# GpSimd rotates q and k of the first layer from two biased copies made by ScalarE

## What is computed

```python
def rotate_half(x):                       # pairs (even, odd) -> (-odd, even)
    return stack((-x[..., 1::2], x[..., ::2]), -1).reshape(x.shape)

xn = layernorm(x)
# layer 1: causal attention, 16 heads of 16, rotary position embedding
Q, K, V = (heads(xn @ W.T + b) for W, b in ((Wq, bq), (Wk, bk), (Wv, bv)))
Q = Q * cos + rotate_half(Q) * sin
K = K * cos + rotate_half(K) * sin
attn = softmax(where(causal, Q @ K.T / 4, -inf)) @ V
# and a gated low-rank mixture: router top 2 of 32, rank 16 each
x = x + attn @ Wo.T + bo + moe(xn)
xn = layernorm(x)
# layer 2: no bias, no rotation; scores times a 0/1 mask (masked keys keep weight exp(0)); a linear
# branch on a second normalisation with the signs of the weights
x = x + attn2(xn) + (layernorm(xn) @ sign(W).T) * scale * gamma + beta
```

## Time and profile before

| | before |
|---|---|
| median of 3 runs | 1581.62 us (1579.21 to 1581.71) |
| the profiled execution | 1581.71 us, its span 1580.0 us |
| instructions | 26931 |
| TensorE matmul busy | 1498.6 us (95%) |
| TensorE weight load busy | 794.9 us (50%) |
| VectorE busy | 1138.0 us (72%) |
| ScalarE busy | 853.8 us (54%) |
| GpSimd busy | 239.0 us (15%) |
| granted TensorE clock, mean | 0.977 of 2.4 GHz |

### The profile page before, as it was taken

One profiled execution on the slowest core, in us unless ns is written; L12 is line 12 of the kernel. 1 busy time (PEld: TensorE's weight loads), 2 busy tenths in 40 slices (PEclk: granted clock), 3 DMA queues, 4 the chain that ended last, 5 costly groups with the idle time before them and its releaser, 6 DMA issues.

```text
span 1580.0 us, 26931 instructions
## 1 busy us (share of the span) xinstructions
PE 1498.6 (95%) x10398; PEld 794.9 (50%) x10398; DVE 1138.0 (72%) x2546; ACT 853.8 (54%) x1661; POOL 239.0 (15%) x196
## 2 busy tenths in 40 slices
PE   4599999999999999999999999999999999999998
PEld 3345445564546544554445644556444554446444
DVE  7788887777675677567887768877776677785851
ACT  1115545556665755666355445454756576664674
POOL 6211202002011302013020021110302131201000
PEclk9779999999999999999999989999999999999999
DMA  5114030030304022230400502004021300304000
GB/s 181 40 41 82 2 81 2 2 81 2 81 2 81 2 43 41 50 85 1 81 2 2 134 1 64 19 1 81 2 48 36 77 6 2 82 2 107 3 2 27
DMA packets 44094, 66.27 MB, mean 42 GB/s; under 512 B 7328, under 2 KB 18880, under 8 KB 43968
## 3 DMA queue, kind: packets, MB, share of 16 engines
q1 hardware_dynamic: 40800, 63.77, 18.1%
q10 hardware_dynamic: 3168, 0.79, 0.2%
HBM read 9.23 MB, written 4.19 MB: 8 GB/s over the span
## 4 chain that ended last, share of the span: by engine, by line
PE 85%; DVE 7%; ACT 4%; issue 2%; POOL 1%; DMA 0%; ACTq 0%; DVEq 0%; POOLq 0%
PE WB L1033 25%; PE O L1178 18%; PE WB L1133 16%; PE ST L1158 15%; PE ST L1161 3%; PE WB L1136 3%; ACT PT L739 3%; PE WB L1186 2%; DVE mxa L971 1%; DVE rope_b L871 1%; PE WB L1194 1%; PE WB L1058 1%; PE WB L1099 1%; DVE veps L825 1%; DVE mxb L971 1%
## 5 line engine op out<-in xcount | busy, mean ns | idle before, releaser
L739 ACT ACTIVATE PT<-ST 128x512 f32<-128x512 f32 (+1 forms) x1216 | 634.5, 578 | 394.0 <-PE ST L1161 292.1
L971 DVE TENSOR_REDUCE mxa<-WB 128x1 f32<-128x512 f32 (+3 forms) x864 | 531.6, 664 | 145.7 <-PE WB L1136 97.3
L1133 PE MATMUL WB<-KS,QS 96*128 96x512 bf16 (+3 forms) x1536 | 436.2, 332 | 7.3 <-DVE attn L1005 4.3
L1158 PE MATMUL ST<-QS,KS 99*128 99x512 bf16 (+3 forms) x1536 | 429.4, 329 | 12.1 <-ACT PT L739 9.7
L1178 PE MATMUL O<-PT,Vaug 128*17 128x512 f32 (+3 forms) x3072 | 323.0, 494 | 7.2 <-ACT PT L739 4.3
L1158 PEld LDWEIGHTS ST<-QS,KS 99*128 99x128 bf16 x1536 | 144.2, 98 | 210.4 <-ACT PT L739 118.9
L971 DVE TENSOR_REDUCE mxb<-WB 128x1 f32<-128x384 f32 (+3 forms) x352 | 213.6, 635 | 36.9 <-PE WB L1136 36.1
L1133 PEld LDWEIGHTS WB<-KS,QS 96*128 96x128 bf16 x1536 | 146.0, 99 | 186.4 <-DVE mxa L971 55.3
L1136 PE MATMUL WB<-negmask,identb 128*128 128x128 bf16 x1024 | 199.8, 222 | 0.0
L1161 PE MATMUL ST<-negmaskT,identb 128*128 128x128 bf16 x1024 | 197.5, 220 | 0.0
L608 POOL TENSOR_TENSOR proj<-proj,parts 128x512 f32<-128x512 f32 x64 | 74.1, 1161 | 457.5 <-ACT parts L699 457.4
(11 more groups left out here) (139 smaller groups left out, 1351.9 us busy)
## 6 DMA issues: line engine op xcount, KB each, us to landing
QS<-parts SPq DMA_DIRECT2D x96, 256.0 KB, 5.0
KS<-parts SPq DMA_DIRECT2D x96, 256.0 KB, 5.0
x<-in_x SPq DMA_DIRECT2D x4, 1024.0 KB, 5.6
out<-x SPq DMA_DIRECT2D x8, 512.0 KB, 2.9
QS<-nmT ACTq DMA_DIRECT2D x32, 24.0 KB
w_q<-in_w_q SPq DMA_DIRECT2D x2, 256.0 KB, 6.1
w_k<-in_w_k SPq DMA_DIRECT2D x2, 256.0 KB, 6.0
cos<-in_cos SPq DMA_DIRECT2D x1, 512.0 KB, 5.5
```

Of the source, the lines that this page charges most:

```text
L739: act.activation(PT[:, q % PT_SLOTS, j:j + n, 0:wd], src, ACT.Exp, scale=float(SCALE[STAGES[k][1]])).then_inc(exp_done.sem, 1)
L971: dve.tensor_reduce(dst, bank, AX.X, ALU.max).then_inc(emptied, 1)
L1133: mm = pe.matmul(bank[:, q * wd:(q + 1) * wd], QS[0:KR, h + qb * P:h + (qb + 1) * P], KS[0:KR, h + seg * BANK:h + seg * BANK + wd], start= ...
L1158: mm = pe.matmul(ST[:, o + i * wd:o + (i + 1) * wd], KS[0:KM, h + kb * P:h + (kb + 1) * P], QS[0:KM, h + q0:h + q0 + wd], start=True, stop ...
```

## The change

28 of the 32 units of the first layer, all but the first four of k = 0 (`ROTATED`), go another way. ScalarE makes two copies of the bank, both with the bias added: one to proj, one to rope_b in two instructions of 64 partitions, crossed over; then the bank is free. GpSimd multiplies rope_b by sin and proj by cos, waits for both, and subtracts them into proj (the sine table has its sign by the half of partitions it is read from, so the addition becomes a subtraction). `first` of the unit waits for this on a new semaphore, `rotated`. As there is one rope_b, ScalarE's copies of a unit wait for the rotation of the unit before. Nothing is removed from VectorE's code: it keeps the first four units. The planner gets the new steps with costs of `ac(512) + 1200` = 1802 ns for ScalarE and 3550 ns for GpSimd.

```diff
--- before.py
+++ after.py
@@ -79,9 +79,15 @@
 W_KINDS = ("wz", "fold", "xT", "qk", "router", "v", "hU", "gT", "ffn", "later", "max", "rows", "out", "aT", "wo")
 
 
+
+ROTATED = [(k, c) for k, (_, l) in enumerate(STAGES) if l == 0 for c in range(NW) if k or c >= NW // 2]
+
+
 def emptier(step):
     if step[0] in EMPTIES_SECOND and STAGES[step[1]][1] == 1:
         return EMPTIES_SECOND[step[0]]
+    if step[0] == "qk" and step[1:] in ROTATED:
+        return "act"
     return EMPTIES.get(step[0], "dve")
 
 
@@ -148,9 +154,17 @@
             due = at(0.1 + 0.03 * c) if ot == 0 else at(0.5 + 0.05 * (c - 4))
             land = [("sp", ("stack", k, 0))] if ot else ([("sp", ("stack", k - 1, 1))] if k else [])
             job("pe", ("qk", k, c), mm(1024, 4) + 60, due, [("act", ("xT", k, 2 * hf + 1)), ("sp", ("weights", 0))], PE_LAG)
-            job(emptier(("qk", k)), ("qk", k, c), 3100 if l == 0 else ac(512), due,
-                [("pe", ("qk", k, c))] + ([("pool", ("third", k, c - 2))] if c > 1 else [("pool", ("third", k - 1, NW - 2 + c))] if k else []))
-            job("act", ("first", k, c), 640, due, [(emptier(("qk", k)), ("qk", k, c))] + land)
+            slot = [("pool", ("third", k, c - 2))] if c > 1 else [("pool", ("third", k - 1, NW - 2 + c))] if k else []
+            done = (emptier(("qk", k, c)), ("qk", k, c))
+            if (k, c) in ROTATED:
+                i = ROTATED.index((k, c))
+                used = [("pool", ("rope",) + ROTATED[i - 1])] if i else [("dve", ("qk", 0, NW // 2 - 1))]
+                job("act", ("qk", k, c), ac(512) + 1200, due, [("pe", ("qk", k, c))] + slot + used)
+                job("pool", ("rope", k, c), 3550, due, [done])
+                done = ("pool", ("rope", k, c))
+            else:
+                job(done[0], done[1], 3100 if l == 0 else ac(512), due, [("pe", ("qk", k, c))] + slot)
+            job("act", ("first", k, c), 640, due, [done] + land)
             job("pool", ("rest", k, c), 1180, due, [("act", ("first", k, c))])
             job("act", ("second", k, c), 640, due, [("pool", ("rest", k, c))])
             job("pool", ("third", k, c), 1180, due, [("act", ("second", k, c))])
@@ -459,6 +473,7 @@
         moe_logits = Signal(sem("moe_logits"))
         moe_exp = Signal(sem("moe_exp"))
         suffix_ok = Signal(sem("suffix_ok"), 6)
+        products, rotated = sem("products"), sem("rotated")
         negmax_parts = Signal(sem("negmax_parts"), NG)
         negmax_in = Signal(sem("negmax_in"), NG, step=16)
         st_full = Signal(sem("st_full"), NG * NEX)
@@ -602,6 +617,19 @@
                 row = brow[:, 1 if STAGES[k][1] == 0 else 2, :].unsqueeze(1).broadcast_to([P, NT, D])
                 pool.tensor_tensor(xs, xs, row, ALU.add).then_inc(biased.sem, 1)
 
+            def rotate(k, c):
+                kind, ot, hf = chunk(c)
+                tok = slice(hf * BANK, (hf + 1) * BANK)
+                done = ROTATED.index((k, c))
+                if done == 0:
+                    pool.wait_ge(w_in["qk"], W_IN["qk"])
+                pool.wait_ge(*empty(("qk", k, c)))
+                pool.tensor_tensor(rope_b[:, :], rope_b[:, :], sin[:, tok], ALU.mult).then_inc(products, 1)
+                pool.tensor_tensor(proj[:, c % 2, :], proj[:, c % 2, :], cos[:, tok], ALU.mult).then_inc(products, 1)
+                pool.wait_ge(products, 2 * done + 2)
+
+                pool.tensor_tensor(proj[:, c % 2, :], proj[:, c % 2, :], rope_b[:, :], ALU.subtract).then_inc(rotated, 1)
+
             def first_rest(k, c):
                 kind, ot, hf = chunk(c)
                 pool.wait_ge(*part1.upto(k, c + 1))
@@ -637,7 +665,7 @@
                 pool.tensor_tensor(ev[:, :, :], later_v[:, g * GH:(g + 1) * GH, :, :].rearrange("p h n v -> p (h n) v"),
                                    e_all[:, g, :].unsqueeze(2).broadcast_to([P, GH * NT, VA]), ALU.mult).then_inc(ev_ready.sem, 1)
 
-            run = {"wmax": largest_weight, "bias": bias, "rest": first_rest, "third": third_part,
+            run = {"wmax": largest_weight, "bias": bias, "rope": rotate, "rest": first_rest, "third": third_part,
                    "suffix": suffix_sum, "ev": later_terms}
             for s in ORDER["pool"]:
                 run[s[0]](*s[1:])
@@ -665,6 +693,21 @@
                     act.wait_ge(*part3.upto(k, c - 1))
                 else:
                     act.wait_ge(*part3.upto(k - 1, NW - 1 + c))
+                if (k, c) in ROTATED:
+                    kind, ot, _ = chunk(c)
+                    bank = bank_of(("qk", k, c))
+                    i = ROTATED.index((k, c))
+                    if i:
+                        act.wait_ge(rotated, i)
+                    else:
+                        act.wait_ge(*empty(("qk", 0, NW // 2 - 1)))
+                        act.wait_ge(w_in["first"], W_IN["first"])
+                    act.activation(proj[:, c % 2, :], bank, ACT.Identity, bias=bcol[:, kind, ot:ot + 1])
+                    for to, at in ((0, P // 2), (P // 2, 0)):
+                        half = slice(at, at + P // 2)
+                        ins = act.activation(rope_b[to:to + P // 2, :], bank[half, :], ACT.Identity, bias=bcol[half, kind, ot:ot + 1])
+                    ins.then_inc(bank_empty["act"], 1)
+                    return
                 act.activation(proj[:, c % 2, :], bank_of(("qk", k, c)), ACT.Copy).then_inc(bank_empty["act"], 1)
 
             def values(k, i):
@@ -689,7 +732,10 @@
 
             def first_part(k, c):
                 kind, ot, hf = chunk(c)
-                act.wait_ge(*empty(("qk", k, c)))
+                if (k, c) in ROTATED:
+                    act.wait_ge(rotated, ROTATED.index((k, c)) + 1)
+                else:
+                    act.wait_ge(*empty(("qk", k, c)))
                 if c == 4:
                     for turn in lane:
                         act.wait_ge(*turn.upto(k, 3))
```

## The result

The changed kernel takes 1565.82 us (median of 4 runs, 1565.65 to 1566.95), the kernel before beside it 1581.44 us (1579.21 to 1581.71): a ratio of 0.9906 [0.9889, 0.9923], 15.6 us faster. The forecast was 1577.5 us; the result lies inside the range, near its fast end and near rival (a)'s 1563. The profiled execution is one of 1565.65 us with a span of 1563.9 us.

A forecast was written before the change was run, and what follows sets the result against it. TensorE was taken as the bound, with 85% of the chain of waits; other engines count only by making it wait. The terms -6.4 - 3 + 4.8 + 0.4 = -4.2 us gave 1577.5 us, range 1563 to 1591 (8 in 10).

The forecast's parts named there:

- rival (a): VectorE was the hidden brake: start-up -6 us, whole excess -12.8 us, ScalarE's copies free; 1563 us, chance 0.18.
- ScalarE's bursts: Three extra copies in a row per unit, 24 in stages 0, 3, 4, at 0.2 us each: +4.8 us (0 to +16.8).
- Contention: GpSimd's added work holds some small VectorE instructions of the splits in stages 0, 3, 4: +0.4 us.
- VectorE's relief: Stages 0, 3, 4: VectorE loses 24 us of rotations each, TensorE's weight loads wait less: -6.4 us (0 to -12.8).
- the half: Only half the excess of weight-load waits counted as time, since loads also idle while the previous matmul streams: -6.4 us.
- 12.8 us of excess waits: Large VectorE rows of weight-load waits: 37.4 us in stages 0, 3, 4 against 24.6 us for three stages without rotations.
- equal ST rows at 51 and 64% of ScalarE: ST waits of 27.3 us (stages 1, 2) and 32.6 us (3, 4): ScalarE's busy share doesn't by itself set TensorE's waits.
- The start-up: Before the first exponential, c = 7's projection moves later and VectorE goes on with maxima: -3 us (0 to -6).
- rival (b): Slower: each of 24 copy bursts on ScalarE costs 0.7 us beyond the ST banks; +7.8 us, 1589.5 us, chance 0.20.
- The cover of GpSimd's chain: Chain to the stack some 2.3 us longer a unit, covered by 16.4 us before the k = 5 transfer: no cost.
- (c): Nothing comes of it: VectorE's time was off the path, its waits pass to ScalarE; 1581 us, chance 0.15.
- (d): GpSimd holds VectorE's two-input split instructions some 0.9 us each in stages 0, 3, 4: +11 us, 1593 us, chance 0.05.

The follow-up runs named there:

- the loads alone: Kernel before, rotation still on VectorE, plus ScalarE's three copies and GpSimd's three operations for each of 28 units on unread buffers: 1589.98 us, ratio 1.0071.
- VectorE refilled: Changed kernel plus three VectorE reductions with unread result for each of the 28 moved units: 1588.37 us, ratio 1.006.
- the kernel planned with 3400 ns: Kernel before with the planner's duration for VectorE's rotation at 3400 instead of 3100 ns, so only orders differ: 1581.14 us, ratio 1.0008.
- k = 0 alone: Kernel before with only the last four units of k = 0 rotated on GpSimd, the others on VectorE: 1576.16 us, ratio 0.9977.
- replanning with 3.95 us: Changed kernel with planned durations as measured, GpSimd's step 3950 instead of 3550 ns and ScalarE's copies 130 ns more: 1567.51 us, ratio 0.9915.
- k = 1: Kernel before with only the eight units of k = 1 rotated on GpSimd, the others on VectorE: 1583.84 us, ratio 1.0025.

## Why the prediction was right in sign and off in size

The forecast was -4.2 us and the time moved by -15.6 us. That it lies in the range is partly luck: the range's fast end was rival (a)'s 1563 us, and (a)'s terms did not come true one by one.

The runs give the terms by themselves, roughly. In the sum of the forecast ScalarE's bursts were +4.8 us; they measured +7.4 (interval 4.1 to 8.5). Contention was +0.4 us; GpSimd's presence measured some +3 to +5. VectorE's relief, start-up included, was -9.4 us; the changed kernel lies 1565.8 - 1590.0 = -24.2 us below the kernel with the loads alone and 1565.8 - 1588.4 = -22.6 us below the one with VectorE refilled. So three terms were too small, the gain by far the most.

**The mis-sized term is VectorE's relief, and the step that failed in it is the half.** I took 12.8 us of excess waits and half of them, -6.4 us, as time, because a load also waits while the matmul before it streams. The excess itself was read from the large rows only; all rows give 21.3 us before and 4.7 us after. And stages 3 and 4 together became 12.5 us shorter, net of bursts, where the forecast had -6.4 + 4.8 + 0.4 = -1.2 us for all three stages. (Stage 0's 4.4 us are hardly a gain, with 3.2 us more in the start.) Three things were outside the sum:
- *Waits in ScalarE's name were in part VectorE's.* I read equal ST rows at 51 and 64% of ScalarE as a matter between TensorE and ScalarE. With VectorE refilled the ST row rose from 30.9 to 35.5 us, of which an order alone can make 2 us. Late maxima empty a bank late, TensorE comes late to everything in its order, and has less in hand when it must wait for an exponential. This chain is my reading; the row is what was shown.
- *The clock.* In 45 runs of the unchanged kernel before, beside the experiments, those with a mean granted clock of 0.977 (six) took 1581.8 us on average, those with 0.982 (two) 1577.7 us: 0.8 us for each 0.001. The profiled before had 0.977 and the profiled after 0.982, which is some 4 of their 16 us. By the traces, stages 3 and 4 had 20.5 us at half clock before and 6.8 us after; half of the difference, 6.9 us, is the most that it can account for of their 12.5 us (5.1 of the 6.4 us in stage 4). My sum priced holes at their length only. Whether the relief of VectorE brought the faster clock is not shown: the kernel planned with 3400 ns, its VectorE unrelieved, has the same 3.4 us at half clock in stage 4.
- *Against it,* VectorE got back 17 of its 83 us, 9 of them in the gating's and 3.4 in L976's small instructions. I had priced this at 3 us, in the splits alone.

**The start-up** was wrong as a mechanism. The transpose of the first maxima starts at 118.72 us, where it started at 118.41; the projection that moved away was replaced by others. The first exponential comes at 127.9 us, and TensorE has 342 matmuls behind it then, 310 before. Its idle time moved, the time of start and stage 0 together went from 322.3 to 321.1 us. With k = 0 alone the same stretch took 316.2 us, so something was to be had there, 3.4 of the 6.1 us of it by the clock (34.1 us at half clock instead of 40.9, an estimate). In the changed kernel stage 0 has 10.2 us at half clock, where k = 0 alone has none; this is within what an order changes.

**The bursts:** 7.4/28 = 0.26 us each, below the 0.38 us from which rival (b) would have decided; the copies in that run read SBUF and took 721 and 711 ns, a little more than the real ones. Of the ST waits of over 1 us in the changed kernel one, of 1.05 us, has such a triple within 2 us ahead of it. Their length was short by 0.3 us of 2.05: no row before showed a copy with a pointer operand, and I took the plain copies' overlap. L705 and L708 take 686 and 683 ns, L711 597 ns. The Trainium skill (ScalarE: Activation LUTs, What ACT_TABLE_LOAD costs) gives 93 ns for a pointer operand. The trace agrees: the differences are 89 and 86 ns. What the prediction made of it was added up wrong: half of 0.28 us over 24 bursts is 3.4 us and not some 2; its sum didn't use it.

**The cover of GpSimd's chain** was looked for at the wrong consumer. I checked the stack's transfer, 16.4 us ahead of need, and priced the longer chain at nothing. The consumer that shows is ScalarE's queue: 17.2 us of waits for the rotation. That a unit's 2 us less on GpSimd are worth 8.7 us over 28 units says that the step was not covered. I had named the exponentials behind that wait and let the planner's 3.55 us settle it. The real step takes 3.84 us, and replanning with 3.95 us did not help.

**The rivals.** (a) comes nearest: VectorE was the brake, its time of 1563 us 3 us off, but by other terms than it names (no gain at the start, bursts not free). (c) is out: the refilled VectorE takes the whole gain back. (d)'s mechanism is there and its price wrong: a few microseconds, because it met the gating's small instructions and a few splits, not every one. One sentence of the forecast covered it ("if VectorE's small instructions are often near 1 us"): L950's mean is 711 ns.

## What to carry to other kernels

When an in-order engine that feeds the bound one is relieved, price the relief from all of the bound engine's waits and its clock, not only from the waits in the relieved engine's name: here 84 us of VectorE were worth about 23 us, more than twice the 9.4 us that I had counted. A step that moves to a slower engine is covered only if its next in-order consumer has slack; look at the queue that waits for it, not at the final transfer. Test a part inside the whole before cutting it out: k = 1 lost 4.6 us alone, where one split met GpSimd at a bad moment, and nothing in company. And sum all rows of a kind of wait: the chosen ones gave 12.8 us of excess, all of them 21.3 us.

## What the runs showed of the hardware

- GpSimd's products and differences of two f32 operands took 1275 to 1282 ns for 128x512, its splits, whose second operand is bf16, 1163 to 1165 ns, and copies of one input 620 ns.
- VectorE's prefix sums, both inputs in SBUF, took up to 1402 ns instead of 425 beside GpSimd's products and splits, and such an instruction took 0.80 us beside its one-input copies alone. A VectorE instruction with one input in SBUF (L1030, f32 to bf16, 128x32) took 1.19 us beside a product, where it takes 178 ns in the kernel before (median). Its reductions of the maxima, with one input from PSUM, stayed as they were: 684 ns before and 683 ns after for 128x512.
- ScalarE's copy with a bias from a column took 684 ns, without one 597 ns; on 64 partitions it took the same 683 ns as on 128.
- Between executions of the same code the mean granted clock went from 0.977 to 0.982, and the time was 4 us shorter with it.
